# The stem's layer-norm variance: a quadratic form of the four inputs in place of 32 squared channels

## The reference, cut to what matters

```python
h = layer_norm(x @ fc0_w + fc0_b, ln0_g, ln0_b)     # 3 values -> 32 channels, per pixel
# layer_norm: (h - mean) * rsqrt(var + 1e-5) * g + b, over the 32 channels
```

## Time and profile before

| what | value |
|---|---|
| median of 3 runs | 3481.48 us |
| span of the profiled execution | 3453.0 us |
| PE, ACT, DVE, POOL busy in it | 91%, 64%, 69%, 61% |
| stem, first matmul to the last step's work | 15.8 to about 451 us |
| busy from 0 to 450 us: PE, DVE, ACT, POOL | 375.93, 250.87, 228.18, 147.39 us |
| granted TensorE clock from 0 to 450 us; over the span | 0.83; 0.944 |

### The profile page before, as it was taken

How to read it: one execution, slowest core, us unless ns; L and a number is a source line. 1 busy time by engine, 2 the same in 40 slices (tenths; PEclk the granted TensorE clock), 3 DMA queues, 4 the chain that set the end, 5 groups by cost and what they waited for, 6 DMA issues and landing times. The chain is left out here.

```text
span 3453.0 us, 190330 instructions
## 1 busy us (share of the span) xinstructions
PE 3139.1 (91%) x80446; PEld 2088.4 (60%) x80446; DVE 2388.5 (69%) x3761; ACT 2210.1 (64%) x3645; POOL 2118.3 (61%) x1147
## 2 busy tenths in 40 slices
PE   6988879999979999979999968999999986999998
PEld 3444457777757777757777743444444434777776
DVE  6555548888848888848888834444444435999996
ACT  4555537777737777737777726777777773655664
POOL 2333338999938999939999924444444443666664
PEclk8888879999989999989999979999999997999998
DMA  3343345555545555445555441211111211000000
GB/s 97 113 114 115 109 149 171 176 176 175 164 140 174 176 176 176 157 139 177 177 177 177 157 128 50 58 54 57 54 57 54 57 29 41 14 13 13 13 13 9
DMA packets 215259, 369.33 MB, mean 107 GB/s; under 512 B 115906, under 2 KB 132994, under 8 KB 214866
## 3 DMA queue, kind: packets, MB, share of 16 engines
q1 hardware_dynamic: 203458, 353.53, 32.8%
q10 hardware_dynamic: 7920, 10.03, 0.9%
q0 software_dynamic: 3744, 3.84, 0.7%
HBM read 209.59 MB, written 157.71 MB: 106 GB/s over the span
## 5 line engine op out<-in xcount | busy, mean ns | idle before, releaser
L1438 POOL TENSOR_TENSOR rstd<-var,mhalf 128x16 f32<-128x16 f32 x512 | 1526.1, 2997 | 703.1 <-DVE var L1213 697.9
L1213 DVE TENSOR_REDUCE var<-sq 128x16 f32<-128x528 f32 x384 | 403.4, 1051 | 81.1 <-ACT sq L885 81.1
L1227 DVE TENSOR_TENSOR zt<-ps,rstd 128x512 f32<-128x512 f32 x512 | 345.5, 684 | 81.2 <-POOL rstd L1438 75.0
L885 ACT ACTIVATE sq<-ps 128x512 f32<-128x512 f32 x512 | 287.9, 596 | 138.4 <-PE ps L533 121.1
L603 PEld LDWEIGHTS ps<-d,hp 128*32 128x32 f32 x24576 | 292.7, 111 | 131.9 <-ACT hp L897 98.9
L603 PE MATMUL ps<-d,hp 128*32 128x48 f32 x24576 | 345.2, 209 | 23.3 <-ACT hp L897 15.7
L533 PEld LDWEIGHTS ps<-cwl,hc 64*64 64x64 f32 x16384 | 274.0, 140 | 136.7 <-issue 130.4
L516 PE MATMUL ps<-zb,ex 48*128 48x512 f32 x1024 | 300.6, 663 | 45.6 <-issue 16.4
L544 PEld LDWEIGHTS ps<-dyi,gt 64*48 64x48 f32 x16384 | 234.8, 126 | 155.3 <-issue 143.4
L1057 ACT ACTIVATE a<-ps,fc1b 128x1024 f32<-128x1024 f32 x256 | 271.3, 1111 | 76.4 <-PE ps L802 76.4
L533 PE MATMUL ps<-cwl,hc 64*64 64x64 f32 x16384 | 310.0, 227 | 0.0
(11 more groups left out here) (193 smaller groups left out, 5414.7 us busy)
## 6 DMA issues: line engine op xcount, KB each, us to landing
h_scratch<-ho SPq DMA_DIRECT2D x256, 512.0 KB
hc<-h_scratch SPq DMA_DIRECT2D x256, 512.0 KB, 4.2
wsb<-in_w SPq DMA_DIRECT2D x64, 288.0 KB, 2.9
gin<-g_scratch SPq DMA_DIRECT2D x252, 72.0 KB
gin<-g_scratch SPq DMA_DIRECT2D x504, 36.0 KB
g_scratch<-hp SPq DMA_DIRECT2D x32, 192.0 KB, 3.9
g_scratch<-hp ACTq DMA_DIRECT2D x32, 192.0 KB, 4.3
tokens<-wsb SPq DMA_DIRECT2D x256, 4.0 KB
```

The costliest lines, as they stand in the source:

```text
L885: nc.scalar.activation(dst, main_ps(s, h, u).rearrange("p (v n) -> p v n", v=2), ACT.Square).then_inc(sq_ready, 1)
L1213: nc.vector.tensor_reduce(dst, src, axis=AX.X, op=ALU.add).then_inc(var_ready, 1)
L1227: nc.vector.tensor_tensor(by_px(zt[h][:, u]), by_px(main_ps(s, h, u)), scale, ALU.mult).then_inc(norm_ready, 1)
L1438: nc.gpsimd.tensor_tensor(rstd[u][:], var[u][:], mhalf[:], ALU.pow).then_inc(rstd_ready, 1)
```

## The change

widen_stem becomes one matmul over all 128 rows, whose moving operand `quad` has 128 columns (2 halves u x 4 inputs x 16 pixels). Its product holds, for each pixel, the 4 x 4 matrix applied to the four inputs. DVE multiplies it by the inputs themselves (`quad_form`: a product of 128 elements a partition, a sum of four, and a maximum with 32 times epsilon on 32 elements) and so has the sum of squares. ACT squares nothing in the stem any more. PE's wait on sq_ready becomes one on `prod_ready`, and lets PE be one step further ahead (`q - 1` where it had to see all squares of the step before). The wait for the inputs in the other layout (`xp_in`) moves from stem_normalise, a step later, to quad_form. Before the first step DVE builds the matrix from the centred weights: a centring of 160 elements in place of 512, then a product, a sum, an addition and a product that spreads it into quad. One constant load more is issued.

```diff
-        loads = [(f0, t["fc0"]), (f0x, t["fc0x"]), ...
+        loads = [(wgram, t["fc0g"]), (pick, t["pick"]), (f0x, t["fc0x"]), ...
...
             def widen_stem(p, i, h):
                 q = 2 * (2 * i + p) + h
-                at_least(pe, sq_ready, 2 * q)
+                at_least(pe, prod_ready, q - 1)
                 if h == 0:
                     pe.wait_ge(xin_in[p], 32 * (i + 1))
-                for u in range(2):
-                    k = slice(64 * u, 64 * u + 64)
-                    last = nc.tensor.matmul(main_ps(STEM, h, u), xin[p][k, h, :], f0[k].rearrange("k c n -> k (c n)"),
-                                            start=True, stop=True, tile_position=(64 * u, 0))
-                last.then_inc(main_ready, 1)
+                nc.tensor.matmul(quad_ps(h), xin[p][:, h, :], quad[:].rearrange("k u a n -> k (u a n)"), start=True, stop=True
+                                 ).then_inc(main_ready, 1)
...
             def stem():                                   # ACT
                 def step(i, p, h):
-                    if behind(i, p, h, 0, 2):
-                        square(STEM, g, h, 0)
-                        square(STEM, g, h, 1)
...
+            dve.wait_ge(consts_ready, len(small))
+            steps = 2 * len(small)
+            nc.vector.tensor_tensor(gprod[:], wgram[:, 1:1 + XCH], wgram[:, 0:1].to_broadcast([128, XCH, C]), ALU.mult
+                                    ).then_inc(small_step, 1)
+            dve.wait_ge(small_step, steps + 1)
+            nc.vector.tensor_reduce(gram[:], gprod[:], axis=AX.X, op=ALU.add).then_inc(small_step, 1)
+            dve.wait_ge(small_step, steps + 2)
+            nc.vector.tensor_tensor(gram[:], gram[:], pick[:, 32:32 + XCH], ALU.add).then_inc(small_step, 1)
+            dve.wait_ge(small_step, steps + 3)
+            wide = [128, 2, XCH, 16]
+            nc.vector.tensor_tensor(quad[:], gram[:].unsqueeze(1).unsqueeze(3).to_broadcast(wide),
+                                    pick[:, 0:32].rearrange("p (u n) -> p u n", u=2).unsqueeze(2).to_broadcast(wide), ALU.mult
+                                    ).then_inc(consts_ready, 1)
...
+            def quad_form(i, p, h):                       # DVE
+                g = 2 * i + p
+                q = 2 * g + h
+                if h == 0:
+                    dve.wait_ge(xp_in[p], 16 * (i + 1))
+                dve.wait_ge(main_ready, q + 1)
+                nc.vector.tensor_tensor(prod[h][:].rearrange("p u k (v r) -> p u (k v) r", v=2),
+                                        quad_ps(h).rearrange("p (u k r) -> p u k r", u=2, r=8), by_input(xp[p], h), ALU.mult
+                                        ).then_inc(prod_ready, 1)
+                dve.wait_ge(prod_ready, q + 1)
+                at_least(dve, root_ready, q - 1)
+                nc.vector.tensor_reduce(sums[h][:], prod[h][:].rearrange("p u k n -> p u n k"), axis=AX.X, op=ALU.add
+                                        ).then_inc(var_ready, 1)
+                dve.wait_ge(var_ready, 2 * q + 1)
+                nc.vector.tensor_scalar(sums[h][:], sums[h][:], C * EPS, None, ALU.max).then_inc(var_ready, 1)
...
                     if old:
                         o = 2 * old[0] + old[1]
                         stem_scale(o, old[2])
-                        for u in range(2):
-                            stem_normalise(old[0], old[1], old[2], u)
+                        stem_normalise(*old)
                     if here:
-                        for u in range(2):
-                            reduce(STEM, g, h, u)
+                        quad_form(i, p, h)
```

More of the change, by code:

```diff
@@ L149, in token_network @@
         cbm = sb("cbm", [64, LAYERS])
-        f0 = sb("f0", [128, C, 16])
-        f0m = sb("f0m", [128, 16])
+        wgram = sb("wgram", [128, 1 + XCH, C])
+        wgm = sb("wgm", [128, 1 + XCH])
+        gprod = sb("gprod", [128, XCH, C])
+        gram = sb("gram", [128, XCH])
+        pick = sb("pick", [128, XCH + 32])
+        quad = sb("quad", [128, 2, XCH, 16])
+        prod = [sb(f"prod{h}", [128, 2, XCH, 16]) for h in range(2)]
         f0x = sb("f0x", [128, 2, 4 * C])
@@ L186, in main_ps, with quad_ps @@
         def main_ps(s, h, u):
-            return ps[:, u if isinstance(s, int) and s in (STEM, LAYERS) else 2 * h + u, :]
+            return ps[:, u if is_last(s) else 2 * h + u, :]
+        def quad_ps(h):
+            return ps[:, h, 0:128]
         t_mid, t_last = ps[:, 4, :], ps[:, 2, :]
@@ L211, in token_network @@
         main_ready = sem("main_ready")
+        prod_ready = sem("prod_ready")
         sq_ready = sem("sq_ready")
@@ L266, in token_network @@
                       (fc2, t["fc2_w"]), (fc2b, t["fc2_b"]), (fc3, t["fc3_w"]), (fc3b, t["fc3_b"])]
-        CONSTS = 19
+        CONSTS = 20
         TNORM = 16
@@ L992, in stem @@
                 act.sem_inc(a_ready, 3 * PAIRS)
+                act.sem_inc(sq_ready, 4 * PAIRS)
             def layer(s):
@@ L1201, in reduce @@
                 dve.wait_ge(sq_ready, n + 1)
[L1203 to L1207, removed]
                 at_least(dve, rstd_ready, n - 1)
@@ L1240, in stem_scale, with stem_normalise @@
                 v.scalar_tensor_tensor(inv[h][:], step[h][:], 1.5, inv[h][:], ALU.add, ALU.mult).then_inc(newton, 1)
-            def stem_normalise(i, p, h, u):
+            def stem_normalise(i, p, h):
                 g = 2 * i + p
[L1245 to L1254, removed]
+                dve.wait_ge(newton, 4 * (2 * g + h) + 4)
+                if h == 0:
+                    at_least(dve, a_psr, g - 1)
+                    at_least(dve, hx_psr, 2 * (g - 1))
+                for u in range(2):
+                    part = (slice(None), u, slice(None), slice(None), slice(8 * h, 8 * h + 8))
+                    nc.vector.tensor_tensor(hx[p][part], xp[p][part],
+                                            inv[h][:, u].rearrange("p (v r) -> p v r", v=2).unsqueeze(1)
+                                            .to_broadcast([128, XCH, 2, 8]), ALU.mult).then_inc(norm_ready, 1)
             def channels(s, which):
@@ L1305, in step @@
                 def step(i, p, h):
-                    g, old = 2 * i + p, behind(i, p, h, 1, 2)
+                    old = behind(i, p, h, 1, 2)
                     here = behind(i, p, h, 0, 2)
@@ L2119, in layouts @@
     cw = np.zeros((2, C, 2, LAYERS, C, 2), np.float32)
-    fc0 = np.zeros((2, 64, C, 2, 8), np.float32)
+    fc0g = np.zeros((2, 64, 1 + XCH, C), np.float32)
+    pick = np.zeros((2, 64, XCH + 32), np.float32)
     for v in range(2):
@@ L2123, in layouts @@
         for r in range(8):
-            fc0[:, 6 * r + 3 * v:6 * r + 3 * v + 3, :, v, r] = f("L0_tok_fc0_w")
-    fc0[:, 48] = f("L0_tok_fc0_b")[:, None, None]
+            fc0g[:, 6 * r + 3 * v:6 * r + 3 * v + 3, 0] = f("L0_tok_fc0_w")
+            for u in range(2):
+                pick[u, 6 * r + 3 * v:6 * r + 3 * v + 3, 16 * u + 8 * v + r] = 1
+    fc0g[:, 48, 0] = f("L0_tok_fc0_b")
+    pick[0, 48, 0:16] = pick[1, 48, 16:32] = 1
+    pick[:, 48, 32 + XCH - 1] = C * EPS
     cw = cw.reshape(128, LAYERS, C, 2)
@@ L2128, in layouts @@
                                    axis=1).reshape(128, LAYERS, 2 * C)
-    out["fc0"] = fc0.reshape(128, C, 16)
     f4 = np.concatenate([f("L0_tok_fc0_w"), f("L0_tok_fc0_b")[None]])
+    fc0g[:, :, 1:] = f4
+    out["fc0g"] = fc0g.reshape(128, 1 + XCH, C)
+    out["pick"] = pick.reshape(128, XCH + 32)
     f0x = np.zeros((128, 2, 2, C, 2), np.float32)
```

6 lines of the change are left out of this document (4 added, 2 removed).

## The result

The changed kernel takes 3491.3 us (median of 16 runs, 3471.9 to 3502.3), the kernel before beside it 3481.0 (16 runs): the ratio is 1.0029, interval 1.0017 to 1.0042. It is slower by 0.3%, where 3452 was forecast. Its profiled execution has a span of 3496.6 us.

A forecast was written before the change was run, and what follows sets the result against it. The stem was bound by a fixed block around POOL's gather train plus release to next train, 27.30 us a couple. 13 + 12 x 1.35 = 29 us off 3453.0 gave a 3424 span, median 28.5 above: 3452 us, range 3422 to 3474.

The forecast's parts named there:

- T to R: Stem, once a couple: start of POOL's eight-gather train to release, when PE's signals are seen; 11.54 us, to stay.
- Rival D: Stem: gathers block only under the profile; 64 steps and the start save 51 us, 3430; chance 0.33 with rival A.
- the pair: Two successive stem steps, h = 0 and h = 1, at full clock: 7.05 us against 8.56.
- the first root: ACT's first root in the stem, at 22.04 us, no longer waits for squares and large sums: about 3 us sooner.
- R to the next train: Stem: release of PE's held signals to POOL's next gather train; 15.76 us before, the steps in it forecast at full clock.
- the caught signal: Stem: the train holds turn_x's signal to hx_copy, pushing channels_out behind the release; 2.1 us a couple, bounds 1.3 to 3.5.
- rival C: Stem: thinner PE work lets half clock last through the steps behind the release; 36 us slower, 3517; chance 0.06.
- rival A: Stem: turn_x's signal gets through or the block is softer; period 23.85, 54 us off, 3427; chance 0.33 with Rival D.
- The base of the sum: Whole kernel: saving taken off the profiled span of 3453.0 us, then 28.5 us added because the runs' median lies above it.

The follow-up runs named there:

- e2: Changed kernel with w_sum, and so the gather train, one step later; 3473.3 us, ratio 0.9995 to the kernel before.
- e3: Changed kernel without its gathers, text embedding tiles filled with zeros; 3290.8 us, ratio 0.9455 to the kernel before.
- e4: Kernel before without its gathers, text embedding tiles filled with zeros; 3339.6 us, ratio 0.9597 to the kernel before.
- e5: Changed kernel with gathers spread, two a step instead of eight a couple; 3297.7 us, ratio 0.9883 to the kernel before.
- e7: Changed kernel with POOL idling 3.1 us ahead of each train; 3298.3 us, ratio 0.9887 to the kernel before.
- g3: Changed kernel itself, timed a third time, on a chip where trains hold up nothing; 3298.9 us, ratio 0.9884 to the kernel before.
- e1: Changed kernel with two unread filler matmuls of 384 columns ahead of each stem matmul; 3514.8 us, ratio 1.0094 to the kernel before.
- f4: Kernel before with gathers spread, two a step, on a chip where trains block; 3452.8 us, ratio 0.9928 to the kernel before.
- e6: Kernel before with gathers spread, two a step, where trains hold up nothing; 3337.5 us, ratio 1.0001 to the kernel before.
- f1: Changed kernel itself again, on another chip where trains block; 3489.3 us, ratio 1.0030 to the kernel before.
- f2: Changed kernel with gathers spread, as e5, on a chip where trains block; 3406.5 us, ratio 0.9791 to the kernel before.
- f3: Changed kernel with POOL idling ahead of each train, as e7, where trains block; 3480.6 us, ratio 0.9997 to the kernel before.
- g1: Changed kernel with spread gathers and w_centre moved behind the second step's pair of gathers; 3297.0 us, ratio 0.9878 to the kernel before.
- h1: Same kernel as g1, run again, again where trains hold up nothing; 3290.0 us, ratio 0.9864 to the kernel before.
- g2: Changed kernel with filler matmuls only in the two steps of each couple behind the release; 3320.7 us, ratio 0.9954 to the kernel before.
- h2: Same kernel as g2, run again, again where trains hold up nothing; 3321.4 us, ratio 0.9955 to the kernel before.

## Why the prediction was wrong, point by point

**The bound.** Right: a fixed block once a couple. T to R was 11.54 us and is 11.9; e2 has 11.46 with another signal in it. Right too that the gathers make it (e3, e4: 136 us). What the forecast took for a trait of the gathers is one of gathers on some chips (e5 to e7, g3). Rival D took the block for a matter of the profile alone; the executions without a block were profiled too, so that alone does not make it.

**The parts.** PE, ACT and DVE came out as costed: product, sum and maximum 0.29, 0.37 and 0.18, from 152.77 to 153.68 us in one row of the timeline, 0.91 against 0.93; the pair 7.06 against 7.05; the first root at 19.09 against 22.04, 2.95 us where 3 were forecast. The 51 us of case D for 64 steps and the start are the 52.5 us of the stem in e3 and e4. The Trainium skill's rule on small instructions (VectorE: DVE Perf Modes, TRN2 errata) did not turn the outcome: three take 0.84 us where two large ones took 2.08.

**The step that failed** is the price of the stretch behind the release, R to the next train. It had its steps at full clock, as if the clock came back where it had before. The profiled stem was to become 29.2 us shorter and became 28.4 longer; of these 57.6, the twelve couples make 47.4. The forecast said 25.95 - 11.54 = 14.4 us; it is 19.1 in the couples of 31.0 us, 17.5 in those of 29.2 and 16.7 in those of 28.6. Its pieces, for the first kind:

| piece | forecast | measured |
|---|---|---|
| the step behind R | 6.15 (2.1 of it for the caught signal) | 8.1 |
| the next one | 3.35 | 5.87 |
| from that matmul of p0h1 to the train | 4.9 | 5.25 |
| train to release | 11.54 | 11.9 |

The first forecast of this table is what is left of 14.4 when 3.35 and 4.9 are taken away. 1.95 + 2.5 = 4.5 of the 5.0 us missed are the two steps at half clock; in the couples of 28.6 us the second is at full clock, and 2.4 us of them are gone. This is what rival C said, and it had been given 0.06. The 4 us a couple in C's sum was shown by no row of before; the runs put 4.5 us in its place, or 2.5 for a step p0h0 (5.87 us at half clock against 3.33 at full). Its period was to be 31.35, and seven couples of thirteen have 31.0; the other six are shorter, so its time of 3517 was not reached.

**The argument against C** was one train, the second of the kernel before, in whose couple PE was back at full clock by channels_out. It carried too much: that train met PE elsewhere, already at half clock (0.50 from 70.11 to 78 us), and left it idle for some 3 us only. The row that spoke for C was there as well. Full clock is not back at R: the two pieces above have 0.64 for the first 6.06 us, which is half clock for 4.4 of them, and 1.00 behind. And before, PE had matmul work inside the block: from 162 us on it was busy without a gap, 4 us ahead of R. In the changed kernel the caught signal leaves it next to nothing there (1.22 us of work from 164.2 to 169.0), and the work without gaps begins only at R. What keeps the clock down for so long is open. Rows of one and the same execution don't settle it: the couple ahead of that of 157.19 has the same matmuls behind its release (138.09), and its clock stayed down all the way to the next train,

```profile
133.50:157.00 23.50, 20.34 (x205) 11.91 (x205) 7.05 (x26) 7.84 (x17) 4.05 (x6) 0.50 0.24 74
```

where in the couple of 157.19 it came back at about 178. That the removed matmul work is the cause is argued, and supported by e1, where added work restored 0.83. It was not separated from the place of the train: e2, which changes only that place, has couples of 26.5 us too. The Trainium skill's account of bursts cut by waits (TensorE: Matmul & The Clock Gate, HAM oscillation), which stood behind C, agrees with the trace: the clock falls anew in every couple, to a mean of 0.60 to 0.76.

**The caught signal** was forecast rightly, and nearly in size. In two couples that run at half clock alike, release to train takes 19.1 us where the signal was caught and 17.5 where it wasn't: 1.6 us, against a forecast of 2.1 and bounds of 1.3 and 3.5. In the three couples of 28.7 to 29.2 us the long wait is xk_copy's, the sign of rival A; its price of 23.85 did not follow, since the steps ran at half clock there too.

**The base of the sum.** The forecast put 28.5 us on the span, as something that lies around it. Each run's time is its span plus 1.8 us. The profiled execution of before was an unusually fast one. A sum made against it should have been set against the median by the ratio or by the saving, and would have ended at 3481 - 29 too; that the base came out the same was luck, and the reason given was wrong.

**What nobody had in the sum.** Between the two landmarks the kernel before takes 2339.9 to 2351.3 us in four kernels (before, f4, e6, e4), and the changed one 2353.7 to 2363.9 in eleven (after, f1, e2, e3, e5, e7, f2, f3, g1, g3, h1); the means are 2346.1 and 2358.3, 12 us more in layers whose instructions the change doesn't touch. With the filler of g2 and h2 it is 2349.9 and 2349.7, and in e1 2354.3. So the net gain where nothing blocks is 37 to 49 us, and not the 52.5 us that the stem wins in e3 and e4. Its cause is open; the placement of code and tiles wasn't tried.

**The change of sign** in ratios to the kernel before: without gathers the change wins 0.9597 - 0.9455 = 0.0142, 49 us. The gathers cost 1 - 0.9597 = 0.0403 in the one kernel (140 us) and 1.0029 - 0.9455 = 0.0574 in the other (200 us), 60 us more. That leaves 10 us of loss, the 0.3% measured.

**What stays open.** Why the trains hold up PE and ACT on the chips of the result, of e1 to e4 and of f1 to f4, and not on those of the other three groups. Each group had its chip once, so chip and session can't be told apart. Every execution here was taken with a profile, so whether the records have a part in it can't be told.

## What to carry to other kernels

Where PE waits in a block once a round, cost the steps behind the block at half clock first, and let full clock be the exception that a row must show; where you remove matmul work there, ask whether the clock will still come back. Before you optimise around a stall, remove it in both kernels and compare: the change's own worth and the stall's price come apart at once. And break up what blocks: two gathers a step in place of eight a couple were worth 83 us to the changed kernel and 29 to the one before, where the trains held PE up.

## What the runs showed of the hardware

- A train of eight indirect DMAs, 0.95 us each and 0.30 apart, keeps PE's small matmuls to about one in 0.7 us and holds signals to ACT for up to 10.2 us ("remote"), on some chips; on three others PE and ACT run on beside it. The kernel before takes 3476 to 3482 us on the one kind and 3336 to 3338 on the other.
- The step p0h0 of the changed stem takes 3.33 us at 2.4 GHz (e3) and 5.87 at 1.2 GHz (after), 2.5 us more.
- One wait of PE of 2.20 us with the half clock behind it made a step 5.1 us longer (g3, 138.95 to 148.40, against 4.38 for its like).
- Behind a block PE stayed at 0.50 for 8.5 us in which it was busy throughout, and in the couple before, where it was busy from 139 to 157 us without a gap, through all of that time:

```profile
169.10:177.60 8.50, 8.50 (x66) 5.49 (x66) 2.13 (x9) 2.96 (x7) 0.00 (x0) 0.50 0.25 78
```
